# A new order for the side units of an attention loop: projections and transposes beside the value products, maxima between the scores

## What is computed

```python
qh = (q @ Wq.T + bq).reshape(bs, -1, H, DK).transpose(0, 2, 1, 3)
kh = (k @ Wk.T + bk).reshape(bs, -1, H, DK).transpose(0, 2, 1, 3)
vh = (v @ Wv.T + bv).reshape(bs, -1, H, DK).transpose(0, 2, 1, 3)
scores = jnp.einsum('bhqd,bhkd->bhqk', qh, kh) / math.sqrt(DK)
attn = jax.nn.softmax(scores, axis=-1)
out = jnp.einsum('bhqk,bhkd->bhqd', attn, vh)
return out.transpose(0, 2, 1, 3).reshape(bs, -1, D) @ Wo.T + bo
```

## Time and profile before

| | |
|---|---|
| median of 3 runs | 783.1 us (775.49, 783.1, 784.4) |
| profiled execution | 776.4 us, of it the span of instructions 774.5 us |
| TensorE busy | 696.1 us, 90% of the span, 12468 matmuls |
| ScalarE busy | 571.9 us, 74% |
| VectorE busy | 585.0 us, 76% |
| GpSimd busy | 455.3 us, 59% |
| mean granted clock of TensorE | 0.952 |

### The profile page before, as it was taken

How to read it: one execution, slowest core, us unless ns; L and a number is a source line. 1 busy time by engine, 2 the same in 40 slices (tenths; PEclk the granted TensorE clock), 3 DMA queues, 4 the chain that set the end, 5 groups by cost and what they waited for, 6 DMA issues and landing times.

```text
span 774.5 us, 33301 instructions
## 1 busy us (share of the span) xinstructions
PE 696.1 (90%) x12468; PEld 450.6 (58%) x12468; DVE 585.0 (76%) x1147; ACT 571.9 (74%) x1143; POOL 455.3 (59%) x491
## 2 busy tenths in 40 slices
PE   6878867398999999999999999999999999997884
PEld 3555542165656666666666666666666666665553
DVE  4677757376778887888888888878878888884498
ACT  3547742287788888888888888888888888887772
POOL 6401152467667667777777766677677777620462
PEclk9889986599999999999999999999999999997997
DMA  7001127627678787877777778786777777750001
GB/s 210 1 2 41 41 62 160 141 82 141 144 140 154 147 151 147 154 139 154 154 174 153 149 150 148 148 157 141 142 154 165 171 142 152 138 108 3 3 0 48
DMA packets 39404, 93.18 MB, mean 120 GB/s; under 512 B 7880, under 2 KB 14536, under 8 KB 39368
## 3 DMA queue, kind: packets, MB, share of 16 engines
q1 hardware_dynamic: 39368, 92.69, 59.0%
HBM read 66.06 MB, written 26.54 MB: 120 GB/s over the span
## 4 chain that ended last, share of the span: by engine, by line
PE 72%; DVE 10%; ACT 8%; issue 6%; DMA 1%; POOL 1%; SPq 1%; ACTq 0%; DVEq 0%; POOLq 0%
PE psum L952 15%; PE psum L979 13%; PE psum L996 11%; PE psum L940 9%; PE psum L1002 8%; PE psum L932 6%; ACT probs L697 4%; PE psum L852 2%; DVE mx L1250 1%; PE psum L838 1%; PE psum L960 1%; DVE k_stack L1391 1%; ACT k L717 1%; DVE rden L1185 1%; DVE stats_f L1315 1%
## 5 line engine op out<-in xcount | busy, mean ns | idle before, releaser
L1250 DVE TENSOR_REDUCE mx<-psum 128x1 f32<-128x500 f32 x672 | 421.4, 672 | 118.2 <-PE psum L952 115.3
L697 ACT ACTIVATE probs<-psum 125x448 f32<-125x448 f32 x768 | 376.0, 543 | 88.0 <-PE psum L979 87.4
L952 PE MATMUL psum<-kh,q_max 64*128 64x500 f16 (+1 forms) x672 | 177.1, 386 | 3.9 <-DVE mx L1250 3.6
L979 PE MATMUL psum<-q_diag,k_stack 64*128 64x112 f16 x3072 | 155.8, 213 | 12.9 <-ACT probs L697 5.6
L996 PE MATMUL psum<-probs,v_ext 125*32 125x112 f32 x3072 | 150.2, 268 | 0.0
L979 PEld LDWEIGHTS psum<-q_diag,k_stack 64*128 64x128 f16 x3072 | 99.2, 95 | 81.3 <-ACT probs L697 49.2
L1002 PE MATMUL psum<-probs,v_ext 125*32 125x112 f32 x3072 | 145.4, 262 | 0.0
L537 POOL CAST kh<-k 128x500 f16<-128x500 f32 x96 | 57.7, 601 | 120.4 <-ACT k L717 120.3
L525 POOL TENSOR_TENSOR c_hl<-c_in,c_hl 128x500 f16<-128x500 f32 x96 | 109.9, 1145 | 7.7
L543 POOL TENSOR_TENSOR kl<-k,kh 128x500 f16<-128x500 f32 x96 | 106.4, 1136 | 0.2
L996 PEld LDWEIGHTS psum<-probs,v_ext 125*32 125x32 f32 x3072 | 74.5, 110 | 31.5 <-issue 21.7
(11 more groups left out here) (147 smaller groups left out, 693.2 us busy)
## 6 DMA issues: line engine op xcount, KB each, us to landing
k_stack<-k_halves SPq DMA_DIRECT2D x192, 187.5 KB, 6.3
c_in<-ctx_in SPq DMA_DIRECT2D x32, 750.0 KB, 5.4
k_halves<-kh SPq DMA_DIRECT2D x32, 375.0 KB, 5.8
k_halves<-kl SPq DMA_DIRECT2D x32, 375.0 KB, 6.3
q_stack<-q_halves SPq DMA_DIRECT2D x32, 64.0 KB, 2.3
q_diag<-mT SPq DMA_DIRECT2D x64, 0.8 KB
q_diag<-mT SPq DMA_DIRECT2D x64, 0.1 KB
out<-x_all SPq DMA_DIRECT2D x8, 112.0 KB
```

The costliest lines, as they stand in the source:

```text
L697: nc.scalar.activation(probs[0:KP, t % PBUF, half * 2 * GC:(half + 1) * 2 * GC], scores[k % RING_AT][0:KP, 0:2 * GC], ACT.Exp, scale=SCALE ...
L952: last = nc.tensor.matmul(bank[:, 0:CH], q_max[u][rows, r * P:(r + 1) * P], kh[u][rows, c * CH:(c + 1) * CH], start=True, stop=True)
L979: mm = nc.tensor.matmul(scores[(2 * t + half) % RING_AT][:, g * PAIR:(g + 1) * PAIR], k_stack[u][rows, g, t * KP:t * KP + P], q_diag[u][ro ...
L1250: dve.tensor_reduce(mx[:, r * KC + c:r * KC + c + 1], bank[:, 0:CH], AX.X, ALU.max).then_inc(mx_done, 1)
```

## The change

The three tables are replaced; no function changes. In every step part "one" (between the two scores) now holds a pair of half maxima, or nothing in step 3. K2, V, T, Z and Y stand in part "two" or "three", directly ahead of the value products or behind them. The order of the maxima puts the full-height one of each chunk beside K2 or V and forms nine pairs of row halves in place of six. The order of the early maxima in the front part changes with `M_ORDER`. ScalarE's copies and VectorE's reductions move with the units, as they follow the same table.

```diff
-M_ORDER = ((3, 0), (0, 0), (1, 0), (4, 0), (5, 0), (2, 0), (6, 0), (0, 1), (1, 1), (4, 1), (5, 1), (2, 1),
-           (6, 1), (3, 1), (0, 2), (4, 2), (3, 2), (1, 2), (5, 2), (2, 2), (6, 2))
-PAIRS = (8, 14, 17, 19, 2, 5)
+M_ORDER = ((0, 0), (4, 0), (3, 0), (1, 0), (5, 0), (2, 0), (6, 0), (0, 1), (4, 1), (3, 1), (1, 1), (5, 1),
+           (2, 1), (6, 1), (0, 2), (4, 2), (1, 2), (5, 2), (3, 2), (2, 2), (6, 2))
+PAIRS = (0, 3, 5, 7, 10, 12, 14, 16, 19)
 SHARED = MB // 2
-PLAN = ((("M1", "M1", "M1", "K2"), ("M1",), ("M1",)),
-        (("M1", "M1", "V"), ("M1", "M1"), ("T",)),
-        (("M1", "K2", "M1", "M1"), (), ("M1", "M1")),
-        (("K2", "Z"), (), ("X",)),
-        (("M2", "V", "M2"), ("M2", "M2"), ("Y",)),
-        (("M2", "V", "M2", "M2"), (), ()))
+PLAN = ((("M1", "M1"), ("M1", "K2"), ("M1", "M1")),
+        (("M1", "M1"), ("M1", "M1"), ("V",)),
+        (("M1", "M1"), ("M1", "K2"), ("M1", "M1")),
+        ((), ("K2", "T"), ("X",)),
+        (("M2", "M2"), ("M2", "V", "Z"), ()),
+        (("M2", "M2"), ("M2", "M2", "V", "Y"), ()))
```

## The result

The changed kernel takes 867.3 us (median of 4 executions, 862.4 to 868.6) against 781.3 for the kernel before (4 executions, 775.5 to 784.4): 1.110 times as long, with a 95% interval of 1.102 to 1.118. Its profiled execution took 862.4 us, with a span of 860.6. Beside each experiment further on the kernel before was run again (medians of 776.0 to 779.7 us), and each ratio there is of fast executions to fast executions of that kernel.

A forecast was written before the change was run, and what follows sets the result against it. TensorE bounds the kernel before; the change exposes the 1.08 us score distance. Fourteen loop pairs at 6.60 us more (92.4), 6.6 ahead and 3 for batch 30 make 102, on 776.4 profiled 878; said 880 us, range 846 to 910.

The forecast's parts named there:

- The distance of 1.08 us: Shortest time from score 2m to score 2m+1, set by the exponential of the first half with three score banks: 1.08 us.
- T, Z, Y: Extra units on TensorE in batches with u = 0, forecast to add 0.49, 0.21 and 0.32 us.
- X to X: Time between starts of the small transpose each loop batch has once: forecast about 20.5 and 21.5 us, before 17.48 and 17.88.
- Short cover: Too little work between two scores: TensorE stands 0.65 us in five steps and 0.87 in step 3, 4.12 a batch.
- V0's copy: ScalarE's copy of V0 behind step 1 delays the next exponential: 0.3 us more in step 2's distance.
- Step 1's wait for VectorE: Step 1's second pair waits for slots of M10 and M11, reduced behind O's copy: 0.23 us, with the release 0.3.
- GpSimd's slack: K2 of step 0 needs a chunk GpSimd splits after V2: 0.3 us of slack; if gone, 0.3 a batch.
- Pairs and changes of shape: TensorE savings a batch: three singles at 0.21 (0.63 us) and seven array shape changes at 0.10 (0.70), together 1.33.
- Outside the steady rounds: Batches beyond the fourteen loop pairs: 6.6 us more for two ahead of the loop, 3 for batch 30.
- The clock rival: TensorE's clock falls because of the loop's gaps; a tenth at 1.2 GHz adds 50 us, 928 in all; chance 0.06.
- The distance rival: The score distance does not set the pace, so savings alone count: 41 us less, 735 us; chance 0.03.
- the one of half the cost: Work behind the stands overlaps better than priced: 1 us a batch, 31 us more, 808; chance 0.06.

The follow-up runs named there:

- doubled maxima: Each maximum between a step's two scores computed twice: in the changed kernel 870.0 us total; in the kernel before 829.4 against 779.7, 1.063 times.
- the run with the late copy: Changed kernel with VectorE's copy of O moved from ahead of maximum 10 to behind maximum 11: 867.0 us.
- the run with five pairs less: Kernel before with five of its six pairs of maxima put on the same row half, by M_ORDER only: 803.0 us, 1.030 times.

## Why the prediction was right, point by point

The distance of 1.08 us was right to 0.01 in five of six steps, and with it the sign and most of the size. By its own steps, for a batch, forecast and measured from score 2m to score 2m+2:

| step | forecast, u = 1 | measured, u = 1 | forecast, u = 0 (T, Z, Y) | measured, u = 0 |
|---|---|---|---|---|
| 0 | 3.46 | 3.47 | 3.46 | 3.46 |
| 1 | 3.59 | 3.71 | 3.59 | 3.73 |
| 2 | 3.76 | 3.57 | 3.76 | 3.57 |
| 3 | 3.08 | 3.06 | 3.57 | 3.49 |
| 4 | 3.29 | 3.28 | 3.50 | 3.39 |
| 5 | 3.29 | 3.40 | 3.61 | 3.56 |

(The steps are those from 428.49 to 470.18, which are two batches' worth; each value is between two starts of score 2m.) That two batches came out at 41.69 us, against 41.96, is in part luck: step 1 (and step 5 with u = 1) took more than forecast and step 2 took less, and much of these errors cancels.

- *X to X.* I gave 20.5 and 21.5 us as signs, and it is 20.93 and 20.75. The signs were misplaced, not the loop: X stands at the end of step 3, so T falls into one interval and Z and Y into the next. For the same reason the 17.88 and 17.48 of the earlier trace rows are not the batches with and without T, Z and Y (Y at 347.52 lies in the second interval). From first score to first score (332.58, 350.65, 367.93) the batches before took 18.07 and 17.28, so that the check of the prices, 17.08 for u = 1, was off by 0.2 and not by 0.4.
- *Short cover.* Right: 47.3 us of idle matmuls in 300, at six scores a batch. The doubled maxima show that it is idle time and nothing else, and the four score banks that it comes from having only three.
- *V0's copy.* The mechanism was right, its size was off: 0.11 and not 0.3. The copy starts 0.10 after the score (442.46 against 442.36) and not 0.2, and the exponential follows at 442.95, 0.49 later and not 0.58, as in these rows the exponential begins 0.10 ahead of the end of the copy (442.46 and 0.59).
- *Step 1's wait for VectorE.* The size was off, 0.45 by the starts (439.70 to 440.36, less 0.21) and not 0.3, and the reason was partly wrong: O's copy isn't on that way, as its run showed. What I had priced too low is the way back, 0.07 (0.3 less 0.23) where the rows of the run with the late copy show 0.25 from the end of a reduction to TensorE's start (446.55 to 446.80).
- *T, Z, Y.* 0.1 too much for Z, which in the earlier trace rows had a change of shape in it.
- *GpSimd's slack* held: from 300 to 600 no matmul of K2 is listed as waiting.
- *The last step with u = 1* has 0.11 more, at the score that opens a round of the loop. The kernel before has 0.17 there (332.58 comes 0.67 after the products of 331.91, 350.65 only 0.50 after those of 350.15). My prices left it out; what it is I didn't try.
- *Pairs and changes of shape.* The pairs' price holds (0.20 each). That of the changes of shape stands only on the starts in the rows; no run changed their number alone.
- *Outside the steady rounds* I had 9.6 us more, and there were 2.5 less. Three parts make this up. The batches ahead of the loop and behind it, the ones meant by the 9.6, took 7.8 more (the first two intervals from X to X and the last). Ahead of the first K2, where both kernels run the same instructions, the changed kernel was 4.4 us earlier: the first transposes there start at 99.57 in the kernel before and at 95.15 in the changed one, and over the twelve profiles of this study, in which nothing ahead of that point differs, they start between 93.2 and 99.6. So I take this part for chance. And in the first rounds of the loop the changed kernel loses 5.8 us less than in the steady ones. There TensorE's matmuls stand for issue in the kernel before (5.6 us in all from 178.9 to 238.2, the two longest below), and only for 0.4 us in the changed one, which stands for its exponentials anyway:

```profile
185.22 0.32 PE L979 MATMUL psum<-q_diag,k_stack 64*128 64x112 f16 x5 [1.31 <-issue]
192.37 0.33 PE L979 MATMUL psum<-q_diag,k_stack 64*128 64x112 f16 x6 [1.31 <-issue]
```

  (Both rows are of the kernel before. One X to X of the first rounds took 27.4 us in the changed kernel with doubled maxima, and 21.2 in the changed kernel itself, so this share may be chance as much as cover; it wasn't tried.)
- *The total.* 878 was meant for the profiled execution, which took 862.4: of these 16 us, 12 lie outside of the steady rounds and 4 in them. The medians are 880 and 867.3.
- *The clock rival* didn't happen: full clock with TensorE busy 83% of the loop in gaps of 0.5 to 0.7 us. The distance rival and the one of half the cost fell with it.

## What to carry to other kernels

Ahead of moving work, look for what spaces two instructions whatever stands between them: here three banks for two writers make a shortest distance of one result's way, one exponential and one release. Work between the two is free up to that distance, and work taken away from there is paid back as idle time. Saving work on the busiest engine (0.20 us for a pair) is worth something only if every slot that it uses comes back in time; with a ring of four and 0.6 us for each slot, three pairs close together cost more than they save.

## What was not expected of the hardware

Four matmuls of 500 columns, two on each row half, in the order upper, upper, lower, lower, took 0.42 us and not 0.63: the idle time shrank by 0.21 where I expected 0.42. Two on the same half do cost 0.20 more than two on opposite halves (the run with five pairs less), so the first of the lower half can't have waited for the second of the upper half. This is inferred from the times; the rows don't name which matmul is which. From the end of a reduction on VectorE to TensorE's next start in that bank it was 0.25 us (446.55 to 446.80), while from the end of an exponential to the next score it is 0.06 (with its 0.54).
